# A graph network in one kernel: the maxima's transposes moved behind the 64-row products of the next group but one

## The chip, the cores and the metric

The kernel runs on one core of a Trainium2 chip. The metric is the device time in microseconds (us). A core has five engines that run their own instruction streams and meet at semaphores: TensorE (PE in the profile; its weight loads are the rows of PEld), VectorE (DVE), ScalarE (ACT), GpSimd (POOL) and SyncE (SP). Sixteen DMA engines move data. TensorE writes to PSUM, eight banks here.

## The reference

A graph network with 50000 nodes of 64 features and 25000 edges, sorted by their destination. First a block of two spline convolutions, then an attention block on the same edges:

```
h = relu(layernorm(x))
conv(x, W, root, bias):
    msg[e] = sum over 4 of 25 knots: basis(edge_attr_2[e], knot) * (x[src[e]] @ W[knot])
    agg[n] = max of msg[e] over the edges with dst[e] = n   (0 where there is none)
    return agg + x @ root + bias
x = x + conv(relu(conv(h, W1, root1, bias1)), W2, root2, bias2)
h = relu(layernorm(x));  d = MLP(edge_attr_3)       # two layers with layernorm and gelu
logits = (h @ Wa)[dst] - (h @ Wb)[src] + d
a = softmax of logits over the edges of a node, per feature
x = x + segment_sum(a * ((h @ Wc)[src] + d), dst)
```

All is computed in float32.

## The kernel before

The edges are taken in G = 49 groups of 512 (four tiles of 128 edges), from the last to the first; the nodes in 49 groups of 1024. The program is written out per engine. A helper `each(engine, step, before, after)` runs `step(g)` for g from -before to G + after - 1: a few steps at either end are written out, and the middle ones stand in a hardware loop of four steps. What an engine does in which order is only the order of the lines in its `step`; engines meet through counters (`Steps`), and `wait(engine, counter, g)` waits until group g's signal has been given.

In one step g of a convolution (function `conv(n)` on each engine, n = 1 or 2):

- GpSimd gathers the rows of group g + 3 (L610, four indirect DMAs in the first convolution and eight wider ones in the second), and in the first convolution scatters the finished rows of a group into a table in memory (L617, four indirect DMAs).
- VectorE spreads every edge's row over five knots (`spread_z`, L1399) and weighs the products (`weigh`, L1419, once for each of the four tiles 0 to 3). It adds these up to messages (`add_pairs`, `add_quads`, `add_last`), and takes the running maximum over the edges of a node (`scan`, L1411, of group g - 1). In the first convolution it also does the layernorm statistics of group g + 2, which begin with L1478, the sum over the gathered rows, and then centre edges (L1498) and nodes (L1503).
- TensorE turns the spread rows (`turn_z`, L1009), multiplies them with the knots' weights (`product_pair(g, 0)` and `product_pair(g, 1)`, L1016, two tiles each), turns the messages (`turn_messages`, L1036), does the nodes (`turn_nodes`, L1047, and `node_roots`, L1058; in the second convolution the edge ends as well, L1067 and L1075), and turns the maxima back (`turn_back`, L1084).
- ScalarE copies turned rows out of PSUM (`evacuate`, L786, for tiles 2 and 3 of the group and for tiles 0 and 1 of the next), squares for the statistics (L816, L821), and copies the turned maxima into the row to be scattered or stored (L841).
- SyncE loads the nodes, and stores their results and, in the second convolution, the maxima (L522).

A product pair has six matmuls with 320 columns: two over all 128 rows for its first tile, then one over the lower 64 rows that ends the first tile and one over the upper 64 rows that begins the second, then two over all 128 rows. Each is one call; a float32 product stands as two records in the trace, so a pair has 12. The first tile is signalled (`prod`) by the lower 64-row product, the second by the last. `turn_back` has four transposes of 64 rows (`agg` lies on 64 partitions).

Of the kernel before, what the change touches and what calls it, by code (L numbers as in the profile page):

```python
# [28 lines left out]
ACT = mybir.ActivationFunctionType  # L29
# [3 lines left out]
C = 64  # L33
K = 5
TPG = 4
# [9 lines left out]
SLOTS = 4  # L45
# [77 lines left out]
def build(nc, a, out):  # L123
# [5 lines left out]
    G = EGROUPS  # L129
# [16 lines left out]
    with ExitStack() as ctx:  # L146
# [283 lines left out]
        def _(sp):  # L430
# [54 lines left out]
            s = cs[1]  # L485
# [31 lines left out]
            def step2(g):  # L517
                if (g - 2).within(G):
                    n = g - 2
                    wait(sp, t["row"], n)  # L520
                    sp.sem_inc(sp_gate, 1)
                    sp.dma_start(M2[bass.ds(n.from_end(G, EG, 1), EG)].rearrange("(t p) c -> p t c", p=P),  # L522
                                 srow[n.slot(SLOTS)][:, :, 0:C]).then_inc(t["mstore"][n.parity], 16)
# [26 lines left out]

            each(sp, step2, 1, 2)

# [25 lines left out]
        def _(pool):  # L578
# [46 lines left out]
            def step(g):  # L625
                if (g + 3).within(G):
                    n = g + 3
                    wait(pool, s["gidx"], n)
                    wait(pool, s["ecen"], n - 2)
                    pool.sem_inc(pool_gate, 1)  # L630
                    gather(n.parity, a["x"], 0, C, s["gathered"])
                if (g - 1).within(G):
                    n = g - 1
                    if n.h is None and n.off == 0:
                        pool.wait_ge(s_zero, 16)
                    wait(pool, s["sidx"], n)
                    wait(pool, s["rowid"], n)
                    wait(pool, s["row"], n)
                    pool.sem_inc(pool_gate, 1)
                    scatter(n, s, T1, third_bound, U)  # L640

            each(pool, step, 3, 1, ahead=3)

# [39 lines left out]
        def _(act):  # L683
# [93 lines left out]
            def conv(n):  # L777
                s = cs[n]

                def step(g):  # L780
# [26 lines left out]
                    if g.within(G):  # L807
                        evacuate(g, 2)
                    if n == 2 and g.within(G):
                        wait_fill(act, s["gathered"], g, 32 * TPG)  # L810
# [22 lines left out]
                    if (g + 1).within(G):  # L833
                        evacuate(g + 1, 0)
                        evacuate(g + 1, 1)
                    if (g - 1).within(G):
                        e = g - 1
                        wait(act, s["at"], e)
                        if n == 2:
                            wait_fill(act, s["mstore"], e - 2, 16)  # L840
                        act.activation(srow[e.slot(SLOTS)][:, :, 0:C],  # L841
                                       bank[5][:, 0:TPG * C].rearrange("p (t c) -> p t c", c=C), ACT.Copy)\
                            .then_inc(s["row"].sem, 1)

                each(act, step, 3, 1, ahead=3)

# [76 lines left out]
        def _(pe):  # L923
# [74 lines left out]
            def conv(n):  # L998
# [13 lines left out]

                def product_pair(g, q):

# [11 lines left out]
                    part(0, 2, 2, low, False, True).then_inc(s["prod"].sem, 1)  # L1026
                    part(1, 2, 2, high, True, False)
                    part(1, 3, 0, whole, False, False)
                    part(1, 4, 1, whole, False, True).then_inc(s["prod"].sem, 1)
# [57 lines left out]

                def step(g):
                    if g.within(G):
                        product_pair(g, 0)  # L1090
                        if n == 2:
                            turn_ends(g)
                        turn_z(g, 2)
                    if (g - 1).within(G):
                        turn_messages(g - 1)
# [11 lines left out]
                    if g.within(G):  # L1107
                        node_roots(g)
                    if (g - 1).within(G):
                        turn_back(g - 1)  # L1110

                each(pe, step, 1, 1)

# [594 lines left out]
```

## Time and profile before

| | us |
|---|---|
| median of 3 runs | 1779.49 |
| lowest and highest | 1778.5, 1780.92 |
| the profiled execution | 1780.99 |
| its span (first to last instruction) | 1779.2 |
| busy: TensorE, VectorE, GpSimd, ScalarE | 1496.6, 1399.6, 1231.8, 742.8 |

The mean granted clock of TensorE is 0.966 of full speed; in both convolutions it is at full speed between 180 and 620 us and between 700 and 1150 us. The profile was taken on one execution; a busy share says how long an engine worked, not whether anybody waited for it. Matmuls are pipelined: one of 0.27 us can follow another after 0.11 us. The chain of waits is followed back from the last instruction, from each to what released it; where no release can be seen it goes to the instruction before on the same engine.

### The profile page before, as it was taken

Reading aid. Unit: us, or ns where it says so; the run is one execution under the profiler, and the core shown is the slowest. Engines: PE = TensorE matmul, PEld = TensorE weight load, DVE = VectorE, ACT = ScalarE, POOL = GpSimd, SP = SyncE. Lnnn points to the kernel's source line nnn. Section 1 sums busy time; section 2 is a strip of 40 time slices with the busy share of each in tenths; the row PEclk is TensorE's granted clock in tenths of the full one; section 3 lists DMA queues with packets and bytes.
Section 4 is the critical chain, followed back from the end, with each engine's and each line's share of the span. In section 5 each row is a group of like instructions: output and inputs, shape, how many; then the busy total and the mean of one; then the engine's idle time right before and its main releaser. Section 6 shows DMA issues by size and latency. Waiting matters only on the chain.

```text
span 1779.2 us, 33700 instructions
## 1 busy us (share of the span) xinstructions
PE 1496.6 (84%) x7834; PEld 998.7 (56%) x7834; DVE 1399.6 (79%) x2704; ACT 742.8 (42%) x1840; POOL 1231.8 (69%) x1207
## 2 busy tenths in 40 slices
PE   3978888888888888999999999996776767776774
PEld 2856566666666655777777777774343333343432
DVE  6259999999999966888888888885676666666674
ACT  3533333333333353333333333335555555555453
POOL 5026777777777747777777777742577777777776
PEclk9989999999999988999999999998999999999898
DMA  8974444444444435877777788763333332323330
GB/s 140 165 106 103 106 102 102 104 107 103 102 103 106 102 77 152 212 208 209 208 204 203 203 205 205 203 180 91 75 70 76 73 69 69 69 68 69 69 75 19
DMA packets 451934, 218.45 MB, mean 123 GB/s; under 512 B 306089, under 2 KB 432058, under 8 KB 451896
## 3 DMA queue, kind: packets, MB, share of 16 engines
q1 hardware_dynamic: 355584, 138.37, 30.7%
q0 software_dynamic: 44864, 65.52, 17.6%
q10 hardware_dynamic: 51448, 14.14, 6.0%
q8 instruction: 14, 0.23, 0.1%
q14 instruction: 24, 0.20, 0.0%
HBM read 128.08 MB, written 92.64 MB: 124 GB/s over the span
## 4 chain that ended last, share of the span: by engine, by line
PE 33%; POOL 12%; issue 8%; DMA 4%; ACT 4%; DVE 3%; POOLq 0%; DVEq 0%; ACTq 0%; SPq 0%
PE bank L1016 18%; POOL gath L610 6%; POOL out_dram L617 5%; PE bank L1009 3%; DMA gath<-M,gidx 3%; PE bank L1058 2%; PE bank L1075 2%; PE bank L1140 2%; PE bank L1047 1%; PE bank L1036 1%; PE bank L1067 1%; PE bank L1084 1%; DVE arena L1630 1%; PE bank L1159 1%; DMA arena<-T 1%
## 5 line engine op out<-in xcount | busy, mean ns | idle before, releaser
L1016 PE MATMUL bank<-Wk,arena 128*128 128x320 f32 (+1 forms) x2352 | 655.2, 464 | 56.2 <-ACT arena L786 56.2
L1016 PEld LDWEIGHTS bank<-Wk,arena 128*128 128x128 f32 (+1 forms) x2352 | 326.9, 188 | 302.3 <-issue 224.3
L610 POOL DMA_INDIRECT gath<-T,gidx x392 | 394.5, 1006 | 131.6 <-issue 125.3
L786 ACT ACTIVATE arena<-bank 128x256 f32<-128x256 f32 (+1 forms) x392 | 168.9, 433 | 310.7 <-PE bank L1009 310.7
L610 POOL DMA_INDIRECT gath<-in_x_dram,gidx x196 | 197.9, 1010 | 138.2 <-ACT gidx L706 79.4
L610 POOL DMA_INDIRECT gath<-M,gidx x196 | 211.1, 1077 | 117.8 <-issue 55.2
L617 POOL DMA_INDIRECT T<-srow,sidx x196 | 213.5, 1089 | 79.3 <-issue 63.7
L1419 DVE TENSOR_TENSOR arena<-bank,A 128x320 f32<-128x320 f32 x392 | 191.6, 489 | 84.2 <-PE bank L1016 80.1
L617 POOL DMA_INDIRECT out_dram<-srow,sidx x196 | 199.0, 1016 | 61.3 <-issue 60.4
L1009 PE MATMUL bank<-ident,arena 128*128 128x128 f32 x980 | 171.7, 274 | 13.1 <-DVE arena L1399 13.0
L1009 PEld LDWEIGHTS bank<-ident,arena 128*128 128x128 f32 x980 | 124.1, 141 | 44.4 <-issue 12.6
L1411 DVE TENSOR_TENSOR_SCAN arena<-ends_cut,arena,bank 64x512 f32<-64x512 bf16 x98 | 123.6, 1261 | 0.9 <-PE bank L1036 0.9
L1159 PE MATMUL bank<-lnq,means 128*128 128x512 f32 x98 | 55.1, 645 | 76.2 <-ACT lnq L910 76.2
L1140 PE MATMUL bank<-arena,Wqk 128*128 128x512 f32 x98 | 60.8, 705 | 56.8 <-DVE arena L1618 56.8
L1058 PE MATMUL bank<-rootpair,nhT 128*128 128x128 f32 x784 | 103.5, 275 | 0.0
L1133 PE MATMUL bank<-DT,spread 128*128 (+1 forms) x392 | 102.9, 386 | 0.0
L1618 DVE SCALAR_TENSOR_TENSOR arena<-bank,arena 128x512 f32<-128x512 f32 x49 | 33.9, 692 | 85.7 <-ACT arena L917 85.7
L1058 PEld LDWEIGHTS bank<-rootpair,nhT 128*128 128x128 f32 x784 | 95.4, 192 | 0.3
L803 ACT ACTIVATE arena<-bank 128x512 f32<-128x512 f32 x49 | 29.4, 600 | 154.7 <-PE bank L1067 154.7
L1399 DVE TENSOR_TENSOR arena<-lnc,a0r 128x320 f32<-128x320 f32 x196 | 93.5, 479 | 0.0
L893 ACT ACTIVATE arena<-bank 128x512 f32<-128x512 f32 x49 | 29.3, 597 | 145.1 <-PE bank L1150 145.1
L1133 PEld LDWEIGHTS bank<-DT,spread 128*128 128x128 f32 x392 | 72.7, 196 | 29.0 <-issue 23.6
(212 smaller groups left out, 2665.8 us busy)
## 6 DMA issues: line engine op xcount, KB each, us to landing
T<-arena SPq DMA_DIRECT2D x96, 272.0 KB
arena<-T SPq DMA_DIRECT2D x48, 544.0 KB
T<-zero ACTq DMA_DIRECT2D x1, 13281.2 KB, 97.6
B<-arena SPq DMA_DIRECT2D x49, 256.0 KB
arena<-B SPq DMA_DIRECT2D x49, 256.0 KB, 3.7
arena<-in_x_dram SPq DMA_DIRECT2D x48, 256.0 KB, 4.0
out_dram<-arena SPq DMA_DIRECT2D x48, 256.0 KB, 3.3
begins_cut<-begins_d SPq DMA_DIRECT2D x49, 128.5 KB, 3.4
```

The source lines that it names most:

```text
L610: pool.indirect_dma_start(out=gath[slot][:, j, k, 0:width], out_offset=None, in_=table, in_offset=bass.IndirectOffsetOnAxis(gidx[slot][:, ...
L617: pool.indirect_dma_start(out=table, out_offset=bass.IndirectOffsetOnAxis(sidx[g.slot(SLOTS)][:, j:j + 1], 0), in_=srow[g.slot(SLOTS)][:, ...
L786: act.activation(ZT[j // 2][:, first:first + chunks, :], bank[j % 2][:, 0:chunks * P], ACT.Relu)\
L1009: tr = pe.transpose(bank[j % 2][:, c * P:c * P + P], Z[g.parity][:, j // 2, (first + c) * P:(first + c + 1) * P], ident[:, :])
L1016: return pe.matmul(bank[2 + r][:, 0:KO], ZT[q][rows, chunk, :], Wk[n - 1][rows, weights].rearrange("p k o -> p (k o)"), start=start, stop= ...
L1058: mm = pe.matmul(bank[7][:, q * P:q * P + P], nhT[:, q * P:q * P + P], root[n - 1][:, :], start=True, stop=True)
L1133: pe.matmul(bank[b + e.parity].rearrange("p (t h e) -> p h t e", h=2, e=P)[:, j], spread[:, j, :], pairs, start=(j == 0), stop=False, skip ...
L1140: pe.matmul(bank[b + g.parity][:, :], W[:, :, :].rearrange("p t c -> p (t c)"), XT[g.parity][:, :], start=False, stop=True, skip_group_che ...
L1159: pe.matmul(bank[7][:, :], means[:, :], squares, start=True, stop=True).then_inc(at["var"].sem, 1)
L1399: V_.tensor_tensor(Z[g.parity][:, j // 2, at_:at_ + KO].rearrange("p (k c) -> p k c", c=C), row.broadcast_to([P, K, C]), w.unsqueeze(2).br ...
L1411: V_.tensor_tensor_scan(agg[g.parity][:, ::-1], ends_cut[g.parity][:, ::-1], bank[4][0:C, ::-1], agg[1 - g.parity][:, 0:1], ALU.add, ALU.max)\
L1419: V_.tensor_tensor(V[:, j].rearrange("p (k o) -> p k o", o=C), bank[2 + j % 2][:, 0:KO].rearrange("p (k o) -> p k o", o=C), A1[:, bass.ds( ...
```

## The change

In both convolutions the four transposes of the maxima are taken one group later and at another place. On TensorE `turn_back(g - 1)` stood at the end of step g; now `turn_back(g - 2)` stands inside `product_pair(g, 0)`, behind its two 64-row products. ScalarE's copy of them stood at the end of its step, for group g - 1; now it stands behind `evacuate(g, 2)`, for g - 2. GpSimd's scatter in the first convolution and SyncE's store of the maxima in the second follow by one group too. All of them get one step more at the end.

```diff
             def step2(g):
-                if (g - 2).within(G):
-                    n = g - 2
+                if (g - 3).within(G):
+                    n = g - 3
                     wait(sp, t["row"], n)
...
-            each(sp, step2, 1, 2)
+            each(sp, step2, 1, 3)
...
-                if (g - 1).within(G):
-                    n = g - 1
+                if (g - 2).within(G):
+                    n = g - 2
                     if n.h is None and n.off == 0:
                         pool.wait_ge(s_zero, 16)
...
-            each(pool, step, 3, 1, ahead=3)
+            each(pool, step, 3, 2, ahead=3)
...
                     if g.within(G):
                         evacuate(g, 2)
+                    if (g - 2).within(G):
+                        e = g - 2
+                        wait(act, s["at"], e)
+                        if n == 2:
+                            wait_fill(act, s["mstore"], e - 2, 16)
+                        act.activation(srow[e.slot(SLOTS)][:, :, 0:C],
+                                       bank[5][:, 0:TPG * C].rearrange("p (t c) -> p t c", c=C), ACT.Copy)\
+                            .then_inc(s["row"].sem, 1)
...
-                    if (g - 1).within(G):
-                        e = g - 1
-                        wait(act, s["at"], e)
...
-                each(act, step, 3, 1, ahead=3)
+                each(act, step, 3, 2, ahead=3)
...
-                def product_pair(g, q):
+                def product_pair(g, q, between=None):
...
                     part(0, 2, 2, low, False, True).then_inc(s["prod"].sem, 1)
                     part(1, 2, 2, high, True, False)
+                    if between:
+                        between()
                     part(1, 3, 0, whole, False, False)
                     part(1, 4, 1, whole, False, True).then_inc(s["prod"].sem, 1)
...
                 def step(g):
+                    def back():
+                        if (g - 2).within(G):
+                            turn_back(g - 2)
+
                     if g.within(G):
-                        product_pair(g, 0)
+                        product_pair(g, 0, back)
...
+                    else:
+                        back()
...
-                    if (g - 1).within(G):
-                        turn_back(g - 1)
-
-                each(pe, step, 1, 1)
+                each(pe, step, 1, 2)
```

TensorE's program in the loop of the first convolution, from the node products (L1058) to the turn of tile 2 (L1009), before; each row is a run of like instructions, x how many, and L113 rows set a register for a wait:

```order
L1058 MATMUL bank<-rootpair,nhT 128x128 x4
L1084 MATMUL bank<-ident,arena 128x64 x4
L113 REGISTER_ALU
L1016 MATMUL bank<-Wk,arena 128x320 x2
L113 REGISTER_ALU
L1016 MATMUL bank<-Wk,arena 128x320 x4
L113 REGISTER_ALU
L1009 MATMUL bank<-ident,arena 128x128 x2
```

The same place now (the node products are L1060, the maxima's transposes L1086):

```order
L1060 MATMUL bank<-rootpair,nhT 128x128 x4
L113 REGISTER_ALU
L1016 MATMUL bank<-Wk,arena 128x320 x2
L113 REGISTER_ALU
L1016 MATMUL bank<-Wk,arena 128x320 x2
L1086 MATMUL bank<-ident,arena 128x64 x4
L1016 MATMUL bank<-Wk,arena 128x320 x2
L113 REGISTER_ALU
L1009 MATMUL bank<-ident,arena 128x128 x2
```

The four transposes have moved past four products: the two whole ones and the two of 64 rows now stand ahead of them.

ScalarE in the same loop, from the copy of the turned maxima (L841) to the squares (L816), before:

```order
L841 ACTIVATE srow<-bank 128x4x64
L706 ISA
L706 ACTIVATE gidx<-srcI 128x4
L796 ISA
L796 ACTIVATE sidx<-thirdI 128x4
L798 REGISTER_ALU
L798 ACTIVATE srow<-rowI 128x4
L113 REGISTER_ALU
L786 ACTIVATE arena<-bank 128x256
L113 REGISTER_ALU
L816 ACTIVATE lnq<-lnc 128x256
```

And now, where the copy is L814 and the squares are L824:

```order
L706 ISA
L706 ACTIVATE gidx<-srcI 128x4
L796 ISA
L796 ACTIVATE sidx<-thirdI 128x4
L798 REGISTER_ALU
L798 ACTIVATE srow<-rowI 128x4
L113 REGISTER_ALU
L786 ACTIVATE arena<-bank 128x256
L113 REGISTER_ALU
L814 ACTIVATE srow<-bank 128x4x64
L113 REGISTER_ALU
L824 ACTIVATE lnq<-lnc 128x256
```

The copy has moved past the index copies and the copy of turned tile 2, to the place ahead of the squares.

GpSimd at the start of the first convolution, up to the loop; gath rows are gathers, T rows scatters, four to a group:

```order
-L610 DMA gath<-in_x_dram,gidx 128x64 x20
-L617 DMA T<-srow,sidx 150000x68 x4
-L610 DMA gath<-in_x_dram,gidx 128x64 x4
+L610 DMA gath<-in_x_dram,gidx 128x64 x24
 L617 DMA T<-srow,sidx 150000x68 x4
```

The gathers of one more group stand ahead of the first scatter.

## Rows read from the trace of the kernel before

**Rows 1.** Busy us (instructions) by stretch: PE, PEld, DVE, ACT, POOL, clock, DMA, GB/s.

```profile
180.00:620.00 440.00, 393.79 (x2194) 269.54 (x2191) 420.59 (x974) 161.25 (x486) 340.62 (x325) 1.00 0.48 104
700.00:1150.00 450.00, 450.00 (x2705) 326.56 (x2704) 388.27 (x698) 156.96 (x451) 338.73 (x337) 1.00 0.80 207
```

**Rows 2.** Chain of waits, second convolution: start us, us, what.

```profile
699.89 0.39 PE bank L1084 x4
...
1178.99 3.09 PE bank L1016 x12
...
1183.30 0.39 PE bank L1084 x4
1183.69 3.29 PE bank L1016 x12
```

**Rows 3.** Chain of waits, end of the first convolution.

```profile
624.03 0.39 ACT arena L786
...
624.54 2.08 PE bank L1016 x8
...
627.84 0.39 PE bank L1084 x4
628.23 2.02 PE bank L1016 x7
```

**Rows 4.** VectorE in time, mid-stage group: start us, us, operation [idle before <-releaser].

```profile
413.19 0.19 DVE L1370 TENSOR_TENSOR a0r<-A,jst 128x36 f32<-128x36 f32 x1
413.65 0.49 DVE L1419 TENSOR_TENSOR arena<-bank,A 128x320 f32<-128x320 f32 x1 [0.28 <-PE bank L1016]
414.06 0.41 DVE L1478 TENSOR_REDUCE jst<-gath 128x4 f32<-128x256 f32 x1
```

**Rows 5.** VectorE in time, an early group.

```profile
130.95 0.18 DVE L1370 TENSOR_TENSOR a0r<-A,jst 128x36 f32<-128x36 f32 x1
131.06 0.48 DVE L1419 TENSOR_TENSOR arena<-bank,A 128x320 f32<-128x320 f32 x1
```

**Rows 6.** GpSimd by line, 181 to 620 us: busy us, mean ns | idle us.

```profile
L617 POOL DMA_INDIRECT T<-srow,sidx x161 | 176.9, 1099 | 49.7 <-issue 46.8 <-ACT srow L798 2.9
L610 POOL DMA_INDIRECT gath<-in_x_dram,gidx x163 | 163.4, 1002 | 49.7 <-issue 49.7
```

**Rows 7.** GpSimd in time, start of the first convolution.

```profile
141.38 1.03 POOL L617 DMA_INDIRECT T<-srow,sidx  x1 [6.29 <-issue]
...
150.85 0.94 POOL L610 DMA_INDIRECT gath<-in_x_dram,gidx  x1 [0.30 <-ACT sidx L796]
```

**Rows 8.** VectorE in time, the gathered rows' sum of an early group.

```profile
153.35 0.42 DVE L1478 TENSOR_REDUCE jst<-gath 128x4 f32<-128x256 f32 x1 [0.51 <-DMA gath<-in_x_dram,gidx]
```

**Rows 9.** GpSimd in time, mid-stage group.

```profile
411.50 0.94 POOL L610 DMA_INDIRECT gath<-in_x_dram,gidx  x1 [0.30 <-issue]
412.76 1.40 POOL L617 DMA_INDIRECT T<-srow,sidx  x1 [0.32 <-ACT srow L798]
414.47 1.00 POOL L617 DMA_INDIRECT T<-srow,sidx  x1 [0.30 <-issue]
```

**Rows 10.** L1084 itself (loads, matmuls: ns min/median/max), loads in time.

```profile
L1084 PEld LDWEIGHTS bank<-ident,arena x392: 134/139/140, 139.1 to 1221.4; 64*128 64x128 f32 x196
L1084 PE MATMUL bank<-ident,arena x392: 222/223/273, 139.1 to 1221.4; 64*128 64x64 f32 x196
...
1007.50 0.32 PEld L1084 LDWEIGHTS bank<-ident,arena 64*128 64x128 f32 x4
```

**Rows 11.** TensorE's matmuls in time, second convolution.

```profile
1007.50 0.46 PE L1084 MATMUL bank<-ident,arena 64*128 64x64 f32 x4
```

**Rows 12.** GpSimd by line, second convolution, 702 to 902 us.

```profile
L610 POOL DMA_INDIRECT gath<-T,gidx x155 | 153.9, 993 | 47.5 <-issue 45.4 <-ACT gidx L711 2.1
```

**Rows 13.** ScalarE in time, first convolution, mid-stage group.

```profile
405.47 0.42 ACT L816 ACTIVATE lnq<-lnc 128x256 f32<-128x256 f32 x1 [0.97 <-DVE lnc L1498]
```

**Rows 14.** SyncE's queue in time, mid-stage group of the first convolution.

```profile
412.91 0.58 SPq L507 DMA_DIRECT2D T<-arena  x1
```

More of the change, by code:

```diff
@@ L835, in step @@
                         evacuate(g + 1, 1)
-                    if (g - 1).within(G):
-                        e = g - 1
-                        wait(act, s["at"], e)
[L839 to L843, printed above, removed]
-                each(act, step, 3, 1, ahead=3)
+                each(act, step, 3, 2, ahead=3)
             act.wait_ge(s_w, WEIGHTS)
```

## The prediction

> **What bounds the kernel now.** I read the busy shares by stretch first, then the chain of waits, then single engines around the places that the change touches. The kernel has three large stages: the first convolution (to about 658 us), the second (about 680 to 1215 us) and the attention stage. The change touches the first two.
>
> In the second convolution TensorE is busy 450 us out of 450 [rows 1], and the chain runs on it alone: in each group it passes the four transposes of L1084 (0.39 us) and the first product pair behind them (3.29 us), while the second pair, which has no 64-row work ahead of it, takes 3.09 us [rows 2]. The first and the last L1084 piece of the chain stand at 699.89 and 1183.30 us, 45 pieces and so 44 periods: 10.99 us a group. This stage is bound by TensorE.
>
> The first convolution is different. TensorE is busy 393.79 of 440 us, VectorE 420.59 [rows 1]. At the 10.86 us a group that GpSimd's rows give below, that leaves TensorE some 1.1 us of waiting in each. The chain at the end of this stage is a ring of three engines: ScalarE's copy of the turned rows (L786), the last eight records of the second pair, then the node products, L1084 (0.39), and then seven records of the next first pair until VectorE may weigh them [rows 3]. VectorE's share of the ring: in a mid-stage group its L1370 starts at 413.19 and the L1419 behind it at 413.65, 0.46 us later; in an early group, where TensorE's product had long been there, the same two stand 0.11 us apart (130.95, 131.06) [rows 4, 5]. So VectorE waits 0.35 us per group for the first product, and has hardly any other gap.
>
> GpSimd is the third party there. Its 324 indirect DMAs between 181 and 620 us take 176.9 + 163.4 us and the gaps before them 49.7 + 49.7 us, almost all the fixed gap of 0.30 us: 439.7 / 324 x 8 = 10.86 us per group, the whole group [rows 6]. And its gathers are only just in time: an early reduce (L1478) sat until a gather ended that was issued at 150.85 us and let go at 153.35 [rows 7, 8]; 2.5 us after the issue at 411.50 is 414.00, and the reduce of that group starts at 414.06 [rows 4, 9].
>
> **The change, part by part.** *TensorE, removed.* At the group's end L1084 goes: 0.39 us, and the first pair behind it drops from 3.29 to the 3.09 us of the pair behind 128-row work, 0.20 us: together 0.59 us [rows 2].
>
> *TensorE, added.* The four transposes run between the 64-row products and the fifth product of the pair, and the switch from 64 to 128 rows that follows is paid there already. Four weight loads span 0.32 us with 0.139 each, so they follow one another at (0.32 - 0.14) / 3 = 0.06 us; the four matmuls span 0.46 with 0.223 each, 0.08 us apart [rows 10, 11]. Four of them cost between 4 x 0.06 = 0.24 and 4 x 0.08 = 0.32 us. The larger figure has the gap of a switch in it, so I take 0.25. Net gain on TensorE: 0.34 us per group, with 0.27 as the near bound. If each load lay bare ahead of its matmul, 4 x (0.06 + 0.14) = 0.80 us would be added: a loss of 0.21. The upper bound is 0.59, if the four cost nothing at all.
>
> The rows show that loads and matmuls of L1084 overlap: four of each lie within 0.46 us, though all use the same 64 rows [rows 10, 11]. The Trainium skill (TensorE: Matmul & The Clock Gate, on packing small matmuls) says that a weight load overlaps with a matmul in flight only when its row group differs. By that rule the first load would wait for the end of the low product and the gain would be 0.34 - 0.14 = 0.20 us per group. The trace contradicts it for L1084 itself, so I keep it as a rival.
>
> *Second convolution.* TensorE is the bound, so 45 groups x 0.34 = 15.3 us come off [rows 2]. What is late next? GpSimd: 155 gathers in 153.9 + 47.5 us, 8 of them in 10.40 us, while it was not held back [rows 12]. The new group is 10.65 us, so it keeps up by 0.25. Everything else that TensorE waits for in this stage had been ready (no idle in 450 us), and all distances within its program but the moved one stay.
>
> *First convolution.* The first product is signalled before the moved transposes, so it comes 0.59 us earlier for VectorE, more than the 0.35 that it waits. Its ceiling: 0.35 x 44 groups (49 less some five at the ends, where the engines are out of step) = 15.4 us, plus the 0.51 us stall at 153.35 [rows 4, 5, 8]. The second product is signalled about 0.25 us later relative to the first, but between the two VectorE does L1478 and six more operations, so it is not waited for.
>
> *ScalarE.* The copy of the maxima moves from the end of the group to behind the third turn's copy. In the first convolution ScalarE then sits 0.97 us idle ahead of L816 [rows 13]; the copy of a larger turned tile takes 0.39 us of the chain [rows 3], so this one fits. If it did not, ring and group would grow by what is over. Its reader of the transposes (L841) no longer makes it wait, since the transposes stand ahead of the turn whose copy comes before it.
>
> *GpSimd and SyncE.* The scatters of a group now follow one gather group later: at the start four gathers run ahead of the first scatter. Before, GpSimd idled 6.29 us ahead of that scatter with the gather queued behind it [rows 7]; four gathers at 1.30 us, 5.2 us, fill this. So gathers gain a lead of about 5 us, once. Behind it GpSimd is still busy all the time. Its period may stay 10.86 us, or fall to 8 x 1.30 = 10.4 if scatters lose their excess: the first of four takes 1.40 us against 1.00 for the next, with SyncE's store L507 issued 0.15 us into it [rows 9, 14]. The gain of the stage is the smaller of VectorE's 15.4 and 5.2 + 44 x (10.86 - period): 5.2 for 10.86, 12.2 for 10.7, 15.4 from 10.6 on. The store will still meet some scatter or gather, mostly elsewhere in the row, so I take 10.7: 12 us, with the early stall 12.5. In the second convolution SyncE's store of the maxima (L522) waits for a row that is one group older at that point of its queue, so it waits less, and the loads behind it are issued no later.
>
> *Sum.* 15.3 + 12.5 = 27.8 us off the profiled execution's 1781.0 gives 1753.2. That execution stands 1.5 us above the median of the runs, 1779.5, so the forecast is 1751.7, rounded to 1752.
>
> **Rivals.** *A: GpSimd holds the first convolution.* For it: no idle beyond the fixed gap, gathers in time by 0.1 us; once VectorE runs against the landing again, scatter and store L507 meet as before. Against it: the scatters' excess should not stay whole while the phases drift. Period 10.86: 5.2 + 0.5 + 15.3 = 21.0 off, 1758.5; with no use of the lead 1763.7.
>
> *B: the loads of the moved transposes are not ahead.* 0.20 us per group: 9.0 in the second convolution, 21.5 in all, 1758.
>
> *C: slower.* Each of the four transposes waits for its own load, and the array runs empty between. It decides from the point at which the four cost over 0.59 us. At 0.80 us the second convolution loses 45 x 0.21 = 9.5 us; in the first, TensorE has 1.1 us of slack and the first product is still early, but GpSimd's period may eat that gain: 1779.5 + 9.5 = 1789. Against it: four of them take 0.39 us of the chain today, switch included.
>
> *D: the change does nothing in the second convolution,* since GpSimd or the gathers' landing takes over: only 12.5 off, 1767. Against it stands the 10.40.
>
> **How the numbers follow.** Forecast (both stages gain, 24 to 32 us off): 68 in 100. A: 16. B: 5. D: 4. C: 4. Nothing measurable for another reason: 3. The range goes from both ceilings, 15.9 + 45 x 0.35 = 31.7 off (1747.8), with 3 us for the spread of the switch costs, to A with no use of the lead (1763.7) and 2 us: 1745 to 1766. A change of 0.2% (3.6 us) is about what can be told from none. Faster 0.93, same 0.03, slower 0.04.
>
> **What the profile after would show.** In the second convolution a TensorE piece of the first pair of about 3.1 us less its split, no L1084 behind the node products, and groups of 10.65 us; 10.8 speaks for B, over 11.0 for C. In the first, L1370 to L1419 0.11 us apart and groups of 10.5 to 10.7 us. If VectorE instead sits ahead of L1478 for the gather in the later groups, GpSimd has taken over, and its period is the stage's. If the moved transposes span more than 0.6 us from the last 64-row product to the next 128-row one beyond what they did before, the TensorE term is wrong. If the first stage gains under 5 us while no engine waits for GpSimd, my reading of the ring is wrong.

## The result and the profile after

The changed kernel takes 1747.7 us (median of 6 runs, 1746.7 to 1754.4) where the kernel before takes 1779.0 (6 runs, 1777.1 to 1781.9): a ratio of 0.983, interval 0.981 to 0.9845. It is faster by 31 us; 1752 was predicted, with a range of 1745 to 1766. The profiled execution took 1748.64 us, span 1746.8.

Where the time went is read from VectorE's scan, the one instruction that stands once in each group of both convolutions. These are its first and last records of each stage after the change (start us, us, engine line, operation):

```profile
132.59 1.26 DVE L1417 TENSOR_TENSOR_SCAN arena<-ends_cut,arena,bank 64x512 f32<-64x512 bf16 x1
...
630.84 1.27 DVE L1417 TENSOR_TENSOR_SCAN arena<-ends_cut,arena,bank 64x512 f32<-64x512 bf16 x1 [0.18 <-PE bank L1038]
...
677.65 1.26 DVE L1417 TENSOR_TENSOR_SCAN arena<-ends_cut,arena,bank 64x512 f32<-64x512 bf16 x1
...
1185.84 1.27 DVE L1417 TENSOR_TENSOR_SCAN arena<-ends_cut,arena,bank 64x512 f32<-64x512 bf16 x1
```

The same four records of the kernel before:

```profile
134.59 1.26 DVE L1411 TENSOR_TENSOR_SCAN arena<-ends_cut,arena,bank 64x512 f32<-64x512 bf16 x1
...
648.93 1.27 DVE L1411 TENSOR_TENSOR_SCAN arena<-ends_cut,arena,bank 64x512 f32<-64x512 bf16 x1 [0.18 <-PE bank L1036]
...
695.78 1.26 DVE L1411 TENSOR_TENSOR_SCAN arena<-ends_cut,arena,bank 64x512 f32<-64x512 bf16 x1
...
1219.79 1.26 DVE L1411 TENSOR_TENSOR_SCAN arena<-ends_cut,arena,bank 64x512 f32<-64x512 bf16 x1
```

Between its scans the first convolution takes 498.25 us where it took 514.34, and the second 508.19 where it took 524.01. So 16.1 us came off the first stage and 15.8 off the second. Ahead of the first scan 2.0 us are gone and behind the last one there are 1.6 more, so the rest of the program differs by under a microsecond in sum. The mean period in the middle of the stages (32 and 25 groups) fell from 10.85 to 10.52 us in the first and from 10.99 to 10.64 in the second.

The busy shares by stretch (the first row answers to the first of [rows 1]; the second has an end at 1130 here, since the stage ends earlier):

```profile
180.00:620.00 440.00, 391.58 (x2265) 278.78 (x2266) 431.51 (x1003) 162.03 (x500) 335.40 (x329) 1.00 0.48 106
700.00:1130.00 430.00, 430.00 (x2666) 322.29 (x2665) 382.31 (x691) 149.31 (x443) 331.15 (x325) 1.00 0.80 212
```

In the first convolution VectorE went from 420.59 to 431.51 busy out of 440: it is now the bound. In the second TensorE still has no idle time.

The chain of waits in the second convolution, the answer to [rows 2]:

```profile
986.25 3.09 PE bank L1016 x12
989.34 0.33 PE bank L1009 x3
989.67 0.89 PE bank L1060 x8
990.57 1.82 PE bank L1016 x8
992.38 0.24 PE bank L1086 x4
992.62 1.27 PE bank L1016 x4
993.89 0.44 PE bank L1069 x4
```

The node products (L1060) are followed by the first pair at once. The pair costs 1.82 + 1.27 = 3.09 us, the four transposes in its midst 0.24. Before it was 0.39 + 3.29. That is 0.35 us off a group.

The weight loads of that place, in time (start us, us, engine line, operation):

```profile
991.57 0.30 PEld L1016 LDWEIGHTS bank<-Wk,arena 64*128 64x128 f32 x4 [0.44 <-DVE arena L1439]
991.95 0.53 PEld L1086 LDWEIGHTS bank<-ident,arena 64*128 64x128 f32 x4
992.55 0.84 PEld L1016 LDWEIGHTS bank<-Wk,arena 128*128 128x128 f32 x4
```

And the matmuls there:

```profile
990.67 1.71 PE L1016 MATMUL bank<-Wk,arena 128*128 128x320 f32 x7
992.22 0.40 PE L1086 MATMUL bank<-ident,arena 64*128 64x64 f32 x4
```

The first transpose's load starts at 991.95 us, while the products of the same rows are still running (until 992.38), and its matmul at 992.22. The load is not bare. The Trainium skill (TensorE: Matmul & The Clock Gate, on packing small matmuls) has loads overlap only where the row group differs. By that the group would have gained, by the prediction's estimate, 0.20 us instead of 0.35; the measurement decides against it. The text above that list also lets a load go ahead when it goes to a background weight buffer; no row here shows a buffer, but the times are as that sentence would have them.

VectorE in the middle of the first convolution, the answer to [rows 4]:

```profile
409.28 0.49 DVE L1425 TENSOR_TENSOR arena<-bank,A 128x320 f32<-128x320 f32 x1 [0.19 <-PE bank L1016]
...
411.34 0.68 DVE L1465 TENSOR_TENSOR arena<-bank,bias1r 128x512 f32<-128x512 f32 x1
411.94 0.68 DVE L1452 TENSOR_TENSOR arena<-arena,jst 128x512 f32<-128x512 f32 x1
412.54 0.19 DVE L1376 TENSOR_TENSOR a0r<-A,jst 128x36 f32<-128x36 f32 x1
412.64 0.48 DVE L1425 TENSOR_TENSOR arena<-bank,A 128x320 f32<-128x320 f32 x1
413.05 0.41 DVE L1484 TENSOR_REDUCE jst<-gath 128x4 f32<-128x256 f32 x1
```

L1376 and L1425, which were L1370 and L1419, are 0.10 us apart where they were 0.46. What is left of VectorE's waiting is 0.19 us for the second pair's last product, and that in one group of four: from 181 to 600 us it waits 1.7 us in 9 times where it waited 12.0 us in 48. The reduce (L1484) waits for no gather.

GpSimd at the same place and by line (181 to 600 us), the answers to [rows 9, 6]:

```profile
410.93 1.02 POOL L617 DMA_INDIRECT T<-srow,sidx  x1 [0.30 <-issue]
412.25 1.24 POOL L617 DMA_INDIRECT T<-srow,sidx  x1 [0.30 <-issue]
413.80 0.98 POOL L617 DMA_INDIRECT T<-srow,sidx  x1 [0.30 <-issue]
```

```profile
L617 POOL DMA_INDIRECT T<-srow,sidx x157 | 166.8, 1062 | 47.9 <-issue 47.6 <-ACT gidx L706 0.3
L610 POOL DMA_INDIRECT gath<-in_x_dram,gidx x160 | 156.7, 980 | 48.8 <-issue 48.8
```

GpSimd still has no idle time beyond the 0.30 us between two DMAs, and yet its group is shorter: the first scatter went from 1.40 to 1.02 us, the second from 1.00 to 1.24. Why its durations change is what the later experiments turned out to be about.

### The profile page after: what moved, and what is told of

The parts are those of the page before. It is cut to its first block, busy times and chain, and to the rows that moved or that the text cites. A ratio compares the mean times of both kernels' runs of the same rounds, so it can differ in the third digit from the quotient of the medians.

```text
span 1746.8 us, 33764 instructions
## 1 busy us (share of the span) xinstructions
PE 1471.2 (84%) x7834; PEld 1002.3 (57%) x7834; DVE 1395.1 (80%) x2704; ACT 731.8 (42%) x1840; POOL 1225.4 (70%) x1207
## 4 chain that ended last, share of the span: by engine, by line
PE 34%; POOL 9%; issue 8%; ACT 5%; DVE 4%; DMA 4%; POOLq 0%; DVEq 0%; ACTq 0%; SPq 0%
PE bank L1016 17%; POOL gath L610 5%; POOL out_dram L617 4%; PE bank L1009 3%; PE bank L1146 3%; DMA gath<-M,gidx 2%; PE bank L1077 2%; PE bank L1060 2%; PE bank L1165 1%; DVE arena L1636 1%; PE bank L1049 1%; PE bank L1038 1%; PE bank L1069 1%; DVE arena L1624 1%; ACT arena L915 1%
## 5 line engine op out<-in xcount | busy, mean ns | idle before, releaser
L617 POOL DMA_INDIRECT T<-srow,sidx x196 | 206.7, 1055 | 69.6 <-issue 59.4
L1425 DVE TENSOR_TENSOR arena<-bank,A 128x320 f32<-128x320 f32 x392 | 190.9, 487 | 57.7 <-PE bank L1016 53.6
L1009 PE MATMUL bank<-ident,arena 128*128 128x128 f32 x980 | 171.7, 274 | 12.4 <-DVE arena L1405 12.4
L1009 PEld LDWEIGHTS bank<-ident,arena 128*128 128x128 f32 x980 | 124.1, 141 | 43.4 <-issue 12.6
L1060 PE MATMUL bank<-rootpair,nhT 128*128 128x128 f32 x784 | 103.6, 275 | 0.0
L1060 PEld LDWEIGHTS bank<-rootpair,nhT 128*128 128x128 f32 x784 | 95.4, 192 | 0.3
```

Source lines behind the costliest of these rows:

```text
L617: pool.indirect_dma_start(out=table, out_offset=bass.IndirectOffsetOnAxis(sidx[g.slot(SLOTS)][:, j:j + 1], 0), in_=srow[g.slot(SLOTS)][:, ...
L1009: tr = pe.transpose(bank[j % 2][:, c * P:c * P + P], Z[g.parity][:, j // 2, (first + c) * P:(first + c + 1) * P], ident[:, :])
L1060: mm = pe.matmul(bank[7][:, q * P:q * P + P], nhT[:, q * P:q * P + P], root[n - 1][:, :], start=True, stop=True)
L1425: V_.tensor_tensor(V[:, j].rearrange("p (k o) -> p k o", o=C), bank[2 + j % 2][:, 0:KO].rearrange("p (k o) -> p k o", o=C), A1[:, bass.ds( ...
```

## Experiments

The kernel before took 1782.8 us (median) beside the first seven runs, 1780.3 beside the next two, 1782.2 and 1784.7 beside the last ones. In the profiled executions of all these kernels the first scan stands anywhere between 132.6 and 136.4 us. Gains of a microsecond or two are therefore read from the stages' scans, not from total times.

**Each stage alone.** The change in the second convolution only, and in the first only:

```diff
-                        if (g - 2).within(G):
+                        if n == 2 and (g - 2).within(G):   # n == 1 in the other run
                             turn_back(g - 2)
...
+                    if n == 1 and (g - 1).within(G):       # n == 2 in the other run
+                        turn_back(g - 1)
```

> The change in the second convolution alone; the first is as before. My theory (two separate gains: TensorE's own time in the second, VectorE's wait for the first product in the first): the second convolution's groups take 10.64 us as in the changed kernel, the first convolution's 10.84 as before, and 15 to 16 us come off in all: about 1763. Rival (the gain hangs on one stage alone, or on the later copy and store): all 31 us or nothing.

> The change in the first convolution alone, GpSimd's scatter order included; the second is as before. My theory: first convolution 10.52 us a group, second 10.99, 15 to 17 us off: about 1763. Rival: nothing here, and all of it in the second.

Measured: 1766.2 us for the second alone, ratio 0.991 (0.9886 to 0.9934), and 1765.6 for the first alone, 0.9897 (0.9873 to 0.9922). With the change in the second convolution the first stays at 514.6 us and the second is 508.2, and the other way round 498.5 and 524.0. The stages are independent, each gives half of the gain, and the two halves add up to the whole.

**The distance alone, at the old place.** Transposes of two groups ago, but at the group's end:

```diff
-                        product_pair(g, 0, back)
+                        product_pair(g, 0)
...
+                    if (g - 2).within(G):
+                        turn_back(g - 2)
```

> The transposes, the copy, the scatter and the store are one group later as in the change, but transposes and copy stand at their old place, at the end of the step. My theory (the place beside the 64-row products is what counts, not the later group): L1084 costs 0.39 us and the first pair 3.29 us as before, the second convolution stays at 10.99 us a group, and the first at 10.8 (VectorE waits for the first product as before): 1776 to 1780. Rival (the waits for the scan or GpSimd's early gathers are what was gained): the first convolution falls to about 10.5 us a group and some 15 us come off: 1764.

Measured: 1787.6 us, outside what was expected. VectorE's wait ahead of L1421 stayed (13.6 us in 48 times from 181 to 600 us, where before has 12.0 in 48), the usual period was 10.82 to 10.90 us, and the second stage took 10.99 a group: no gain from lateness. In this one run the first stage lost 4.8 us, at one stall, VectorE's wait for a gather, which also made the next group 2 us longer:

```profile
285.62 0.42 DVE L1480 TENSOR_REDUCE jst<-gath 128x4 f32<-128x256 f32 x1 [3.16 <-DMA gath<-in_x_dram,gidx]
```

The gap between the stages, where the scatters drain, is 51.8 us instead of 46.9. Neither loss is shown to come from the distance: a stall of the same length, 3.16 us, stands in the run inside the second pair below, which has the old distance, and the changed kernel with the new distance has a gap of 46.8. What is shown is that being later by a group gives nothing by itself; the place gives the gain.

**Behind the pair instead of inside it.**

```diff
-                    if between:
-                        between()
                     part(1, 3, 0, whole, False, False)
                     part(1, 4, 1, whole, False, True).then_inc(s["prod"].sem, 1)
+                    if between:
+                        between()
```

> As the change, but the transposes stand behind all six products of the first pair, among 128-row work. My theory has two mechanisms and this keeps one: TensorE pays both switches again (0.59 us instead of 0.25), so the second convolution goes back to about 10.99 us a group; but the first product still comes before the transposes, so VectorE's wait in the first convolution stays away and its groups stay at 10.52 us: about 1763. Rival (one mechanism, less TensorE time, acts in both): both stages fall back to their old periods, about 1778.

Measured: 1764.6 us. The second stage takes 522.1 us, 10.93 a group, and its chain shows why:

```profile
990.09 3.09 PE bank L1016 x12
993.18 0.39 PE bank L1086 x4
993.57 0.58 PE bank L1069 x4
```

The transposes cost 0.39 us again, and the 128-row transposes behind them 0.58 where they take 0.44 behind the pair. The switch is paid for anew. The first stage keeps its whole gain: 497.4 us. This separates the two mechanisms. In the first convolution it is enough that nothing stands between the node products and the first pair; in the second the transposes must share the switch of the 64-row products.

**Inside the second pair.** The same group's distance as before (one), but within the second pair:

```diff
+                    def back():
+                        if (g - 1).within(G):
+                            turn_back(g - 1)
...
-                        product_pair(g, 1)
+                        product_pair(g, 1, back)
```

> The kernel before with one edit: turn_back(g - 1) stands behind the 64-row products of the second pair of the same step; copy, scatter and store keep their group and place. My theory: the second convolution gains the same 0.34 us a group (10.64, 15.5 us in all), since the switches are shared there too. In the first convolution the second pair lies in the ring ScalarE, TensorE, VectorE: the first product still comes 0.34 us earlier, but the last product of the second pair comes 0.25 us later and VectorE waits for it: 10.7 to 10.8 us a group, 2 to 6 us off. In all 1758 to 1762. Rival (any 64-row neighbour does the same everywhere): 1748, as the change.

Measured: 1765.6 us, ratio 0.9902 (0.9885 to 0.9918). The second stage has its full gain (10.64 a group), the first only a third (10.75), as expected. The total is above the 1758 to 1762 that were expected: the first stage is only 2.3 us shorter (512.1), since its second group has a stall of 3.16 us, VectorE's wait for a gather at 157.20 us. VectorE's wait moved to the second pair's last product, the longer one of this kernel:

```profile
411.35 0.49 DVE L1425 TENSOR_TENSOR arena<-bank,A 128x320 f32<-128x320 f32 x1 [0.34 <-PE bank L1016]
...
414.61 0.19 DVE L1376 TENSOR_TENSOR a0r<-A,jst 128x36 f32<-128x36 f32 x1
414.71 0.48 DVE L1425 TENSOR_TENSOR arena<-bank,A 128x320 f32<-128x320 f32 x1
```

**Eight transposes instead of four,** each made twice:

```diff
-                    for j in range(TPG):
+                    for j in (*range(TPG), *range(TPG)):
```

> As the change, but turn_back does its four transposes twice over, to the same places. My theory: behind 64-row products a transpose costs 0.06 us, so four more cost 0.25 us: the second convolution goes from 10.64 to 10.89 us a group and is 11 us longer; the first convolution stays at 10.52, since TensorE has 1.2 us to spare there and VectorE does not wait for what is behind them. About 1759. Rival B of the prediction (each load bare, 0.20 us each): 11.4 us a group in the second convolution, over 1780. Rival (the first stage is bound by TensorE too): its groups 10.77, another 11 us.

Measured: 1760.8 us. The second stage takes 10.879 us a group, 0.241 more for four more transposes, 0.06 each. In the chain the piece is

```profile
992.82 0.49 PE bank L1086 x8
```

and the first stage does not change (10.53), since TensorE has slack there.

**Three scatters instead of four in the first convolution.** The fourth tile's maxima are left out.

```diff
-                for j in range(TPG):
+                for j in range(TPG - 1 if s is cs[1] else TPG):
```

> As the change, but the first convolution scatters only three of its four tiles (the fourth tile's maxima are left out). It takes one indirect DMA, 1.3 us, from GpSimd's 10.52 us a group. My theory (VectorE and its ring set 10.52, GpSimd follows): the groups stay at 10.50 to 10.54 us and GpSimd now idles about 1 us in each beyond the fixed 0.30 us gaps; the end of the stage, where scatters drain, is some us shorter: 1742 to 1748. Rival (GpSimd, without a single idle beyond 0.30 us, is the pacemaker): the groups fall to 10.3 us or less, and 9 us or more come off in the stage.

Measured: 1749.9 us in one run, first stage 10.505 us a group against 10.525. The total is above the 1742 to 1748 that were expected, with its first scan at 136.4 us; the drain was to be some us shorter and is 0.5 (46.3 between the stages). GpSimd does an eighth less and the stage does not notice: GpSimd does not set its period. But nor did it fall idle by 1 us a group as expected; it idles 0.36 us more. The DMAs that are left grew longer (181 to 600 us):

```profile
L611 POOL DMA_INDIRECT gath<-in_x_dram,gidx x160 | 188.1, 1175 | 62.3 <-issue 62.3
L618 POOL DMA_INDIRECT T<-srow,sidx x120 | 133.1, 1109 | 36.6 <-issue 36.0 <-ACT gidx L707 0.6
```

Seven DMAs fill nearly the time of eight; the last gather of a group takes 1.56 to 1.70 us in most groups. So "GpSimd is busy the whole group" says nothing of its pace, and the question became what lengthens its DMAs.

**A combined version.** Behind the pair in the first convolution, within it in the second:

```diff
-                    if between:
+                    if between and n == 2:
                         between()
                     part(1, 3, 0, whole, False, False)
                     part(1, 4, 1, whole, False, True).then_inc(s["prod"].sem, 1)
+                    if between and n == 1:
+                        between()
```

> The changed kernel, with the transposes behind the whole first pair in the first convolution (as in the run that moved them there, 10.496 us a group) and between the 64-row and the fifth product in the second (10.638). If the two stages add as they stood apart, the first convolution takes 44 x (10.525 - 10.496) = 1.3 us less than in the changed kernel: 1746.5 where the changed kernel has 1747.7, within what the runs can tell. If the gain of 0.03 a group in the single look was scatter, the time is that of the changed kernel.

Measured: 1747.6 us (5 runs), ratio to before 0.982 (0.9806 to 0.9835). The first stage has 10.496 us a group, the second 10.638. The 0.03 us a group is there again, but the time can't be told from the changed kernel's 1747.7.

**SyncE's store moved.** In the traces SyncE's store of the T1 rows (L507) is issued 0.15 us into the lengthened scatter before ([rows 9, 14]) and 0.02 us into the one after. Is it the cause?

```diff
                     sp.dma_start(nx[n.parity][0:p, :, 0:C], rows).then_inc(s["nload"][n.parity], 16)
+                if (g - 1).within(G):
+                    n = g - 1
+                    wait(sp, s["out"], n, "out")
...
+                    sp.dma_start(rows[:, :, U:2 * U], no[n.parity][0:p]).then_inc(s["nstore"][n.parity], 16)
...
-                if g.within(G):
-                    wait(sp, s["out"], g, "out")
```

> The changed kernel, with SyncE's store of the T1 rows in the first convolution (L507) one step later in its queue, behind the load L495. Theory (a DMA that SyncE issues while GpSimd issues an indirect one lengthens that one): the second scatter of a group, 1.21 us in the mean of the changed kernel, falls to 1.00, and the one that runs at the new place of the store grows by 0.15 to 0.4 us; the period stays at 10.5 us, since VectorE holds the stage. Rival (the second scatter is longer for its own sake): it stays at 1.2 and no other grows. If GpSimd's period were the pacemaker, the stage would move by 44 times whatever its sum of eight durations changes.

Measured: 1750.8 us in one run, first stage 10.49 us a group. The second scatter fell to 1.00 us, as the theory says; but no DMA grew by 0.15 to 0.4 us where the store now stands. And the version with the transposes behind the pair has the same eight durations, within 4 ns each, with the store at its old place in the queue. The theory's first half had come true for another reason, and the run does not decide.

**VectorE's instruction replaced.** Within the lengthened scatter VectorE's small product a0r starts, both before and after. It is left out of the first convolution here, in the kernel before and in the changed one:

```diff
-                    V_.tensor_tensor(a0r[:, :, :], back_tiles_of(A0, g),
-                                     jy[:, 0:TPG].unsqueeze(2).broadcast_to([P, TPG, KR]), ALU.mult)\
+                    if n == 1:
+                        V_.memset(a0r[:, :, :], 1.0).then_inc(s["a0r"].sem, 1)
```

> The kernel before, with VectorE's a0r product in the first convolution (L1370, two SBUF inputs) replaced by a fill of the same tile with 1.0; the product itself is left out. In the trace of before this product starts 0.42 us into the first scatter of each group, which lasts 1.40 us, and over all runs a GpSimd DMA lasts about 0.97 us plus the product's distance from its start. Theory (GpSimd's DMA stands still while VectorE reads two SBUF operands): the first scatter falls from 1.40 to about 1.00 us; the stage's period stays near 10.86 less at most the 0.1 us by which the fill is shorter, since TensorE's ring holds it, and GpSimd's spare time turns up at another VectorE instruction or as a wait. Rival (SyncE's store L507, 0.14 us into the same scatter, lengthens it): the first scatter stays at 1.40.

> The changed kernel, with VectorE's a0r product in the first convolution replaced by a fill, as in the other run. There the product starts 0.25 us into the second scatter, which lasts 1.21 us. Theory of the shared access: the second scatter falls to 1.00 us, SyncE's store staying where it is; VectorE bounds the stage, so its period falls by the 0.1 us or so that the fill is shorter, 10.52 to about 10.42, unless GpSimd, whose eight DMAs without any lengthening need about 10.3 us, is met on the way. Rival: the scatter stays at 1.2 us.

Measured: 1779.8 and 1743.7 us. In the kernel before, the first scatter stayed at 1.40 us:

```profile
404.12 1.40 POOL L617 DMA_INDIRECT T<-srow,sidx  x1 [0.30 <-issue]
```

So a0r is not the cause. The stage's period is 10.86 us, as before. VectorE's records there show what is in flight when this scatter starts: not a0r but the instruction ahead of it, which also reads two SBUF operands.

```profile
403.94 0.68 DVE L1449 TENSOR_TENSOR arena<-arena,jst 128x512 f32<-128x512 f32 x1
404.58 0.09 DVE L1371 MEMSET a0r<- 128x36 f32 x1
```

It gives way to the next at 404.58, and the scatter ends 0.94 us after that (404.12 + 1.40 = 405.52), about what a whole DMA takes where nothing lengthens it (0.94 to 1.02). In the changed kernel the fill shortened VectorE's group by 0.10 us and the stage's period followed, 10.525 to 10.423, while GpSimd's eight DMAs kept up without idle time. That is the most direct evidence that VectorE bounds the changed first stage.

**One operand instead of two.** In the kernel before, the instruction in flight (L1446) scales the node rows:

```profile
412.59 0.68 DVE L1446 TENSOR_TENSOR arena<-arena,jst 128x512 f32<-128x512 f32 x1
```

Here it is a sum over an axis of length one; the scaling is left out of the first convolution.

```diff
-                    V_.tensor_tensor(nh[:, :, :], nln[:, :, :],
-                                     jy[:, TPG:].unsqueeze(2).broadcast_to([P, NPP, C]), ALU.mult)\
+                    if n == 1:
+                        V_.tensor_reduce(nh[:, :, :], nln[:, :, :].unsqueeze(3), AX, ALU.add)\
+                            .then_inc(s["xn"].sem, 1)
```

> The kernel before, with VectorE's scaling of the node rows in the first convolution (L1446, 128x512, two SBUF operands) replaced by a sum over an axis of length one: the same size and output, one SBUF operand, some 0.67 us; the scaling itself is left out. In the trace of before L1446 is in flight when a group's first scatter starts and ends 0.42 us into it (412.59 + 0.60 against 412.76), and the scatter lasts 1.40 us. Theory (GpSimd's DMA stands still until a VectorE instruction with two SBUF operands that is in flight has ended): the first scatter falls to about 1.00 us. The fill in place of the product behind it left 1.40, as this theory has it. Rival (SyncE's store L507, 0.14 us into the scatter): it stays at 1.40. The stage's period stays near 10.86 us either way if TensorE's ring holds it; where GpSimd then is ahead of its data, its time turns up as another lengthening or as a wait.

Measured: 1778.3 us, the period as before (10.85). VectorE's record, GpSimd's and SyncE's:

```profile
412.68 0.67 DVE L1447 TENSOR_REDUCE arena<-arena 128x512 f32<-128x512 f32 x1
```

```profile
412.86 1.02 POOL L617 DMA_INDIRECT T<-srow,sidx  x1 [0.34 <-ACT srow L798]
...
419.48 1.30 POOL L610 DMA_INDIRECT gath<-in_x_dram,gidx  x1 [0.30 <-issue]
```

```profile
412.99 0.58 SPq L507 DMA_DIRECT2D T<-arena  x1
```

The scatter starts 0.18 us into a VectorE instruction of the same length, and SyncE's store is issued 0.13 us into it, both nearly as before (0.17 and 0.15); beside the reduce it takes 1.02 us in place of 1.40. The store is ruled out: the product L1446 is what lengthened it. That two SBUF operands are enough is not shown, and the changed kernel speaks against it. There VectorE's last addition of the messages (its L1446, another line than the product's) adds two parts of one SBUF tile, and 27 scatters that begin inside it between 181 and 600 us all take 1.02 us:

```profile
221.49 0.47 DVE L1446 TENSOR_TENSOR msg<-arena 128x256 f32<-128x256 f32 x1
```

```profile
221.51 1.02 POOL L617 DMA_INDIRECT T<-srow,sidx  x1 [0.30 <-issue]
```

The products L1446 and L1399 read two tiles, at least one of them broadcast; whether that counts was not tried. Nor are additions always without effect: the fourth gather of the kernel with the reduce takes 1.11 us in the mean, where 0.94 is the least, beside such additions alone. In that kernel the time did not become idle: the second gather now takes 1.30 us in each group. It starts inside another such instruction of VectorE:

```profile
419.44 0.47 DVE L1399 TENSOR_TENSOR arena<-lnc,a0r 128x320 f32<-128x320 f32 x1
419.84 0.17 DVE L1524 TENSOR_SCALAR jst<-jst 128x12 f32<-128x12 f32 x1
```

419.84 + 0.94 = 420.78, which is where that gather ends (419.48 + 1.30). The changed kernel's second scatter fits as well: L1452 gives way at 412.54 us, and 412.25 + 1.24 = 413.49 is 0.95 us later.

## Why the prediction was right, step by step

*The TensorE term, 0.34 us a group:* measured 0.349. All its parts are in the chain: 0.39 gone, the pair at 3.09, the transposes at 0.24 (0.25 taken), and a second measurement of 0.06 for one transpose. The second convolution was to give 15.3 us and gave 15.8. TensorE remained its bound, GpSimd kept up, and rivals B (0.20 us a group), C and D are refuted.

*VectorE's wait, 0.35 us a group in the first convolution:* gone as predicted, L1376 to L1425 at 0.10 us. Of the ceiling of 15.4 + 0.5 us all was reached, 16.1. The run with the transposes behind the pair confirms the reason: the gain comes with the early first product, wherever behind it in the first pair the transposes stand. The run inside the second pair shows the condition, that the second pair's last product does not come later for it.

*GpSimd's period, 10.7 us:* this is the term that was mis-sized. I took 10.86 us for GpSimd's own pace of before and let only 0.16 of the first scatter's 0.40 us of excess go; that gave 12.0 us, 12.5 with the early stall. The stage runs at 10.52 and gave 16.1 with the start. The step that failed is the reading "GpSimd is still busy all the time, so its period bounds the stage". Eight DMAs at the durations that nothing lengthens, four scatters of 1.02, 1.00, 0.99 and 0.98 us and four gathers of 0.99, 0.97, 0.94 and 0.94 us with 0.30 us between, need about 10.25 us. The rest of each group, 0.6 us before and 0.27 after, lies inside the DMAs' spans. Where it was followed up, in the scatters of three kernels and one gather, it is a wait for an instruction of VectorE that reads two SBUF tiles. The first gather of a group in the kernel before is another case: it takes 1.13 to 1.21 us where 0.99 is the least, and begins beside a reduce. A product (L1399) starts 0.90 us into it, near its end; that this lengthens it is a reading of the rows and was not tried. GpSimd so has time to spare that shows as busy: seven DMAs filled 10.5 us with 0.36 us of idle time beyond the fixed gaps, and eight fit into 10.42. Rival A, GpSimd as the bound, is refuted by both runs. The prediction also named SyncE's store as the reason for the excess; the last run shows that it was not.

*The early stall* (0.51 us at 153.35) is gone: between 130 and 181 us VectorE waits only once, 0.2 us, for TensorE. The lead that four early gathers give does not help by itself: the late version at the old place had it and gained nothing. Beside a faster VectorE it may be worth more than this stall: the version inside the second pair, which has no lead, waits 3.16 us for a gather in its second group. The two were not tried apart.

*ScalarE* hid its moved copy: L814 stands at 403.61, straight behind the turn's copy, and still 0.82 us of idle time follow it ahead of L824.

*The sum.* 15.3 + 12.5 = 27.8 us were forecast, 31.9 came in the two stages. The difference is 0.5 from TensorE's term and 3.6 from GpSimd's. A miss among the expectations: the late version at the old place was to lie at the kernel before or slightly under it, and was slower by 5 us. It took one stall for a gather and a longer drain at the stage's end; the changed kernel has the same distance and took neither. Why was not tried, and it was one run.

## What to carry to other kernels

When small work needs another array shape, put it beside work of that shape that is there already: here four 64-row transposes on their own cost 0.39 us and 0.20 more on the products behind them, and 0.24 between 64-row products. Before calling an engine the bound because it shows no idle time, give it less to do, or compare its shortest durations with its mean ones; a duration can hold a wait. And count what stands between the last result of one group and the first product that the next engine waits for: moving it behind that product took away the next engine's whole wait here, 0.35 us a group.

## What the runs showed of the hardware

An indirect DMA that GpSimd begins while VectorE runs the product L1446 takes 1.40 us, and 1.02 with a one-operand reduce of the same length in its place. Its end follows from VectorE's records: 0.94 or 0.95 us after its next instruction starts in the three kernels above, and 0.98 in the kernel before. The Trainium skill (SBUF — State Buffer, Who interferes with whom) says that a VectorE instruction with two SBUF inputs contends with a GpSimd instruction that reads SBUF, and that a reduce never contends, with which the 1.40 us beside the product and the 1.02 beside the reduce agree. It also takes it that such a product does not stall the making of descriptors, which the 1.40 us contradict; beside the addition of two parts of one tile a scatter of 1.02 us is as the page has it.

How far this reaches is open. The two-operand product a0r, which starts only as the one in flight gives way, added nothing: a fill in its place left the 1.40 us. But in the kernel with three scatters a gather of 1.70 us (from 418.55) ran past two such instructions, the second of which began 0.20 us after it. At which points a DMA can be held, and by which instructions, was not measured.

A 64-row transpose between 64-row products costs 0.06 us, the same for the fourth and the eighth, with its load under the matmuls ahead.
